# Self-attention on one core: the third score matmul of a step is issued between the round of ones and the round of values

## The reference, cut to what matters

```python
q, k, v = ...                                  # (B, H, T, DH) = (2, 16, 2048, 32)
z = T * jax.nn.sigmoid(x.mean(axis=1) @ span_w + span_b)
scores = jnp.einsum('bhtd,bhsd->bhts', q, k) / SCALE
scores = jnp.where(causal, scores, NEG_INF)
attn = jax.nn.softmax(scores, axis=-1)
mask = jnp.clip((R + z[:, :, None, None] - dist) / R, 0.0, 1.0)
attn = attn * mask
attn = attn / (attn.sum(axis=-1, keepdims=True) + 1e-08)
out = jnp.einsum('bhts,bhsd->bhtd', attn, v)
```

## Time and profile before

| | us |
|---|---|
| median of 3 runs | 3446.59 |
| lowest and highest | 3441.65, 3451.08 |
| the profiled execution's own time | 3444.47 |
| its span, first to last instruction | 3442.7 |
| TensorE busy in it | 3025.1 |
| VectorE, ScalarE, GpSimd busy | 1885.6, 1057.0, 1005.1 |

### The profile page before, as it was taken

How to read it: one execution, slowest core, us unless ns; L and a number is a source line. 1 busy time by engine, 2 the same in 40 slices (tenths; PEclk the granted TensorE clock), 3 DMA queues, 4 the chain that set the end, 5 groups by cost and what they waited for, 6 DMA issues and landing times. The chain is left out here.

```text
span 3442.7 us, 56565 instructions
## 1 busy us (share of the span) xinstructions
PE 3025.1 (88%) x19622; PEld 1696.3 (49%) x19622; DVE 1885.6 (55%) x2260; ACT 1057.0 (31%) x2524; POOL 1005.1 (29%) x657
## 2 busy tenths in 40 slices
PE   7997899999999999999997799999999777667768
PEld 6885333333333333333332677777777343333345
DVE  4333878787888878787877344444444210000038
ACT  3222244434444444434443222222222101011013
POOL 0001444444444444544444022222222000000013
PEclk9998699999999999999998799999999988888879
DMA  4455412121212212121213411111111749999935
GB/s 147 146 209 183 94 47 66 50 66 50 69 50 56 69 49 70 47 66 50 60 50 84 143 45 60 61 59 59 59 59 63 281 172 421 420 420 420 421 134 163
DMA packets 189972, 450.90 MB, mean 131 GB/s; under 512 B 18254, under 2 KB 55304, under 8 KB 165208
## 3 DMA queue, kind: packets, MB, share of 16 engines
q1 hardware_dynamic: 181543, 437.25, 37.0%
q10 hardware_dynamic: 8240, 11.04, 0.9%
HBM read 364.06 MB, written 83.89 MB: 130 GB/s over the span
## 5 line engine op out<-in xcount | busy, mean ns | idle before, releaser
L537 POOL TENSOR_TENSOR B_em<-B_e,B_mask 128x1024 f32<-128x1024 f32 (+1 forms) x322 | 675.3, 2098 | 756.9 <-ACT B_e L681 715.0
L681 ACT ACTIVATE B_e<-B_pS 128x512 f32<-128x512 f32 (+3 forms) x1288 | 621.6, 533 | 893.6 <-PE B_pS L775 460.0
L594 DVE TENSOR_REDUCE B_mx<-B_pM 128x4 f32<-128x2048 f32 (+1 forms) x320 | 627.4, 1961 | 43.7 <-PE B_pM L734 22.5
L772 PE MATMUL B_pS<-B_qs,B_ks 128*128 128x512 f32 (+3 forms) x1288 | 505.8, 446 | 26.9 <-issue 23.6
L587 DVE SCALAR_TENSOR_TENSOR B_em<-B_mask,B_e 128x1024 f32<-128x1024 f32 (+1 forms) x322 | 352.6, 1095 | 217.3 <-PE B_pN L802 215.5
L772 PEld LDWEIGHTS B_pS<-B_qs,B_ks 128*128 128x128 f32 x1288 | 229.2, 192 | 343.0 <-issue 227.8
L790 PE MATMUL B_pD<-B_e,B_tiny 128*32 128x512 f32 (+3 forms) x2560 | 308.7, 555 | 0.0
L796 PE MATMUL B_pD<-B_em,B_ones 128*32 128x512 f32 (+3 forms) x2560 | 298.7, 539 | 0.0
L802 PE MATMUL B_pN<-B_em,B_v 128*32 128x512 f32 (+3 forms) x2560 | 293.6, 531 | 0.0
L1796 DVE TENSOR_TENSOR E_ug<-E_pT,bT 128x32 f32 x32 | 5.7, 192 | 453.5 <-PE E_pT L1878 453.5
L1886 PE MATMUL E_pY<-ring,E_vT 128*32 128x512 f32 x512 | 91.2, 877 | 115.1 <-DMA ring<-in_L_ffn_e_W_dram 112.7
(11 more groups left out here) (272 smaller groups left out, 4875.0 us busy)
## 6 DMA issues: line engine op xcount, KB each, us to landing
ring<-in_L_ffn_e_W_dram SPq DMA_DIRECT2D x128, 1024.0 KB, 19.4
ring<-in_L_ffn_e_Wg_dram SPq DMA_DIRECT2D x64, 1024.0 KB, 23.8
B_qs<-q_hi SPq DMA_DIRECT2D x72, 256.0 KB, 4.6
B_ks<-k_hi SPq DMA_DIRECT2D x72, 256.0 KB, 4.0
A_xin<-in_x_dram SPq DMA_DIRECT2D x10, 1024.0 KB, 13.3
B_kh<-k_hi SPq DMA_DIRECT2D x36, 256.0 KB, 2.7
B_qh<-q_hi SPq DMA_DIRECT2D x36, 256.0 KB, 3.7
B_qs<-q_lo SPq DMA_DIRECT2D x36, 256.0 KB, 4.5
```

The lines of the kernel that those rows point to most:

```text
L537: nc.gpsimd.tensor_tensor(em[:, f % SLOTS_EM, DVE_HEADS:, w0:], e[:, f % SLOTS_E, DVE_HEADS:, w0:], mask[:, DVE_HEADS:, u0:u0 + BLK - w0], ...
L594: nc.vector.tensor_reduce(mx[:, :, qt, c], pM[:, :, 0:w], AX.X, ALU.max).then_inc(max_taken, 1)
L681: nc.scalar.activation(e[:, f % SLOTS_E, h, w0:], pS[:, h % SBANKS, w0:], ACT.Exp, scale=SCALE).then_inc(exp_ready, 1)
L772: last = nc.tensor.matmul(pS[:, h % SBANKS, w0:], ks[:, kb // NT, h, kb % NT * P:(kb % NT + 1) * P], qs[:, qb, h, w0:], start=True, stop=( ...
```

## The change

`mix` gets a third argument, a function that it calls between the round of ones and the round of values. The loop passes one that issues score 2 of the running step. After the turn only score 3 is left. No instruction is added or removed.

```diff
-            def mix(it, f):
+            def mix(it, f, between):
...
                     nc.tensor.matmul(pD[cols, w0:], ones[:, :], em[:, f % SLOTS_EM, h, w0:],
                                      start=False, stop=final, tile_position=(0, h * DH))
+                between()
                 if first:
                     pe.wait_ge(num_out, it * BPB + qb + 1)
...
                     scores(it, f, (0, 1))
-                    mix(it, f - 2)
+                    mix(it, f - 2, lambda: scores(it, f, (2,)))
                     n, later = unit_of(f)
                     if n == 0 or n - 1 in ENDS:
                         turn(rows_before(it + later, n))
-                    scores(it, f, (2, 3))
+                    scores(it, f, (3,))
                     unit(it + later, n)
```

## The result

| | before | after |
|---|---|---|
| median, us | 3444.12 | 3512.93 |
| lowest and highest | 3436.67, 3451.08 | 3507.16, 3515.13 |
| span of the profiled execution | 3442.7 | 3509.4 |
| self-attention, first to last values round | 1471.7 | 1543.0 |
| the rest of the span | 1971.0 | 1966.4 |

The change makes the kernel slower by 68.8 us, ratio 1.0196 with the interval 1.0173 to 1.0218. The forecast was 3512, on the scale of the earlier median 3446.59: +65, and +68.8 came.

The account below looks back on a forecast made before the run. TensorE, busy 3025.1 of 3442.7 us, was taken to bound the kernel. Terms summed to 8.2 us an iteration; 8 x 8.2 - 0.7 = 65 us, giving about 3512 us, range 3485 to 3535.

Parts of the forecast that it names:

- The plain step: Full width, off-diagonal unit, 10 an iteration: 0.56 us paid, 0.49 given back, +0.07 each, +0.70 an iteration.
- Diagonal: 12 steps with diagonal scores in this step or the next: +0.22 us taken for all, +2.6 an iteration.
- narrow: From a narrow step into a full one (f = 3, 11, 23): +0.38 us each, +1.1 an iteration.
- diagonal-unit steps: Full-width steps with the unit on the diagonal (f = 6, 26, 27, 28, 34): 0.12 us taken, +0.60 an iteration.
- f = 13: Step without a turn where ScalarE copies the sums first, so exponential 2 is as late as now: +0.56 us.
- Steps with a turn: f = 5, 21, 25, 33: at most 0.1 us given back, 0.56 paid, 0.48 taken, +1.9 an iteration.
- Covered steps: f = 4, 24, 39, 40: VectorE's waits hide the price, so nothing; about 0.4 us each without cover.
- the first step: First step after the branch (f = 41 to 2), at granted clock 0.50, 1.2 GHz: +0.7 us an iteration.
- B: Rival: weight loads of scores 2 and 3 are fetched ahead after all; 10 us slower, 3457; chance 0.07 with its surroundings.
- C: Rival, faster: score 2's new place costs 0.33 us as between two scores, no drain; -22 us, 3425; chance 0.07.
- D: Rival: score 2 waits for exponential 0 in its new place and holds values up; given no chance of its own.
- the waits of the score's load for ScalarE: Sign in self-attention: these waits should fall well below 111.5 us while self-attention's time grows by 65.

Follow-up runs that it names:

- the extra score inside: Kernel before plus an unread second copy of score 2 between ones and values in every step: 3596.9 us, 151 us over before.
- the full-width set: The change only in 15 of 40 steps, full-width ones followed by full-width ones; the other 25 keep the order of before: 3456.0 us, ratio 1.0043.

## Why the prediction was right, step by step

**The plain step.** Forecast 4.81 to 4.88, from 0.56 paid and 0.49 given back. Measured 4.89 to 4.90 (f = 12, whose values rounds are narrow, 3.20 after 3.10); the price is 0.56 by the extra score inside, and the borders of the full-width set show 0.54 and -0.47. Of the four intervals named, three came as said (0.97, 0.43, and 0.42 for score 3 to unit). Values to score 3 is 1.00. My list of signs had 0.97 there, but the price had 0.02 more for the round behind score 2, and the list left it out. So the sum of plain steps is 0.83 and not 0.70 by about 0.01 a step.

**Diagonal, narrow and diagonal-unit steps, and f = 13.** Forecast 2.6, 1.1, 0.60 and 0.56; measured 2.60, 1.15, 0.54 and 0.57. Behind a diagonal step, 512 to 384 wide, score 3 to `tiny` is 1.88 (forecast 1.86), and ones to values with score 2 in it is 0.55 longer (forecast 0.56). One value for all diagonal steps was a choice that held in the sum only: their intervals range from 0.09 (f = 20) to 0.33 (f = 7 and 35). That the steps outside the full-width set carry the loss is shown by that set: it has 13 us of 69.

**Steps with a turn.** Forecast 1.9, measured 2.90, and the agreement is worse than that. The term has two parts that I didn't separate. At f = 21 and f = 33 it is 0.53 and 0.50 of the 0.48 forecast. At f = 25 it is 0.01, since the turn's wait takes it up, which I had granted to f = 24 only. At f = 5 it is 1.86, of which 1.6 is the lower clock (7.17, against 5.57 with score 3 ahead of the turn): 13 us in the eight iterations, which no rival held. The earlier trace rows showed me such a stretch after the branch, and I treated it as bound to that place; the same trace has one at f = 25 in two iterations, and I didn't ask what another order would make of such places.

**Covered steps and the branch.** Forecast 0 for f = 4, 24, 39 and 40 and +0.7 for the first step. Measured +0.83 and -0.07. At f = 39 and 40 the intervals grow by 0.46 and 0.09. In 41 the unit comes 0.71 sooner after the last values round, since its wait for the reduction is 2.98 instead of 3.40: the cover, booked one interval later than in my table. Behind the branch ones to values is longer by 0.76 to 0.80 where both kernels are at the lower clock there, as the 0.7 had it. The time in between, from the unit to score 0, is 3.9 to 4.3 us before and 3.6 to 4.2 after. So f = 39 to 41 together are +0.48 where I had +0.7, and the cover was real. At f = 4 and 24 the 0.09 and 0.19 are small, as said.

**The sum.** 8.2 an iteration was 65; measured are 8.9 and 71.3 in self-attention. The stretches outside it came out 4.6 us shorter in this profile, which brings the span to +66.7. No experiment explains those 4.6 us; they are of the size by which executions of one kernel differ. So the forecast is right in mechanism and in the classes that make up two thirds of it, and its agreement to 1 us is partly luck. The median of the kernel before fell from 3446.59 to 3444.12 with a fourth run, and by differences it is 65 against 68.8. And terms cancel: the unforeseen clock stretch at f = 5 (+1.6 an iteration) and the steps that weren't quite covered (+0.8) stand against terms that were too dear, at f = 5 without the stretch, at f = 25 and at the branch (0.2, 0.5 and 0.8).

**The rivals.** B and C fall by the loads: the load of score 2 starts with its matmul at 728.39, after 0.84 us without a load, and ones to score 2 is 0.97. So it is for all 424 full-width scores behind a round in this trace: the load starts at most 2 ns before its matmul. Behind another score a load can be ahead, as the row at 706.04 shows. The Trainium skill's sentence in "TensorEngine Tiling (Array Packing)", section "Key Properties", that a change of mode drains the engine, agrees with the 0.11 and the late loads, though no row shows the engine empty. The one on loads pulled ahead in "TensorE: Matmul & The Clock Gate", section "Step-by-step: what each phase is for", sets conditions, on row groups or a background weight buffer; for full-width scores no load was ahead behind a round. D didn't occur: score 2 waits for nothing in the new place.

**A sign that misled.** I had said that the waits of the score's load for ScalarE would fall well below 111.5 us. They rose to 277.9. In the rows at 729.82 and in the earlier trace rows the same 0.84 us without a load stand once as "issue" and once as a wait for ScalarE: where exponential 2 has just ended, the releaser named is ScalarE, but the engine waited for its own values round, and it would have waited the same without ScalarE. Of the 277.9 us, 226.4 are 270 such waits of 0.8 to 0.9 us, of which the kernel before has none; the other 51.5 are less than half of 111.5, as I had said. The starts of the matmuls were the better test; the total of a wait by releaser was the wrong one.

## What to carry to other kernels

A matmul that is moved to hide another engine's latency should be priced by its new neighbours: between matmuls of another form it pays two changes and an uncovered weight load, here 0.56 us (a full-width score in float32) against 0.33 in its old place, so group by form first. Move only where what comes back of the wait is larger than the difference of 0.23: in a plain step ScalarE cost 0.34, but only 0.16 of it came back. A producer that is made earlier can start beside an engine that it used to follow; look at what else the same semaphore releases, and order the two if they collide. And before a reordering of some tenths of a microsecond, list where the engine stands still for about as long: the clock fell behind such places here, though not behind each.

## What the runs showed of the hardware that was not expected

- VectorE's and GpSimd's multiplications of 128x1024 float32 in SBUF don't overlap: 1.23 and 2.38 us alone; started 0.04 to 0.25 us apart, the second lasts 3.40, whichever it is. Keeping them apart was worth 60 us of 3491 in one pair of kernels and 80 of 3573 in another. VectorE's maximum over a PSUM tile wasn't longer beside GpSimd's multiplication (2.29 against 2.28 us).
- TensorE's granted clock fell from 2.4 to 1.2 GHz for 3.4 us behind a wait of 0.80 us that follows the narrow steps, in eight of eight iterations; with a wait of 0.39 it fell in two of eight, and before the change, with 0.98 at the same place, in none. Neither this wait nor its sum with the next one (in the same order 1.14 to 1.19, 1.02 to 1.04 and 1.08 to 1.14) decides. One such stretch costs about 1.6 us (7.17 against 5.57).
- Two more scores in a row cost 0.55 us together and not 0.66, since their loads start during the first one's matmul (0.11 us behind its start). A score's load behind a round of another form starts with its own matmul, in 424 of 424 cases.
